# Second attention of a four-layer network: one written order of slots, with score, maximum and exponential as separate steps

## The reference, cut to what matters

```
xn = layernorm(x)                                  # 2 x 1024 x 256
q = rope(xn @ Wq.T)                                # 16 heads of 128
k = rope(xn @ Wk.T); v = xn @ Wv.T                 # 4 heads of 128, each for 4 query heads
g = sigmoid(xn @ Wgslc.T) + sigmoid(xn @ Wgswa.T)  # one number per token and head
p = softmax(q @ k.T / sqrt(128) + causal mask)
x = x + (g * (p @ v)) @ Wo.T
```

## Time and profile before

| | |
|---|---|
| median of three runs | 3405.4 us |
| the profiled execution, its own time | 3405.0 us |
| its span, first to last instruction | 3403.2 us |
| second attention, first score to the next stage's first product | 735.89 to 1728.80 us |
| mean granted clock of TensorE, all stages | 0.913 |
| busy: TensorE, VectorE, ScalarE, GpSimd | 2888.8, 1793.9, 912.8, 732.8 us |

### The profile page before, as it was taken

The page is one execution under the profiler, slowest core; times in us unless marked ns, Lnnn a source line. Parts: engine busy times, 40 slices in busy tenths (PEclk is TensorE's granted clock), DMA queues, the critical chain, the costliest instruction groups (busy, mean ns, idle before and its releaser), DMA issues. The chain is left out here.

```text
span 3403.2 us, 34916 instructions
## 1 busy us (share of the span) xinstructions
PE 2888.8 (85%) x13440; PEld 1767.6 (52%) x13440; DVE 1793.9 (53%) x3555; ACT 912.8 (27%) x1644; POOL 732.8 (22%) x796
## 2 busy tenths in 40 slices
PE   5889889989999999999999548899788886759975
PEld 3556545655555455555455425555455555636653
DVE  5565641156665756665711357777577763322223
ACT  2434441023233323332311022222222223212211
POOL 3221210012222312322200102333123334230020
PEclk8999989979999999999999668999799997759987
DMA  4112201030000000000000200000000000411220
GB/s 127 29 30 47 45 19 50 0 122 0 1 1 1 0 1 0 1 1 13 0 0 0 85 6 13 13 10 10 10 13 10 13 24 10 190 63 49 66 71 36
DMA packets 52932, 100.62 MB, mean 30 GB/s; under 512 B 10080, under 2 KB 34784, under 8 KB 51488
## 3 DMA queue, kind: packets, MB, share of 16 engines
q1 hardware_dynamic: 49176, 88.94, 9.2%
q0 software_dynamic: 3072, 8.39, 0.8%
q10 hardware_dynamic: 520, 1.07, 0.2%
HBM read 54.32 MB, written 18.61 MB: 21 GB/s over the span
## 5 line engine op out<-in xcount | busy, mean ns | idle before, releaser
L1133 ACT ACTIVATE back<-ps,front 128x128 f32<-128x128 f32 (+7 forms) x256 | 189.7, 741 | 617.7 <-DVE front L1175 617.6
L1098 PE MATMUL ps<-back 128*128 128x512 f32 x576 | 296.1, 610 | 67.6 <-DVE back L1194 34.2
L778 DVE TENSOR_REDUCE front<-ps 128x1 f32<-128x512 f32 (+3 forms) x384 | 197.5, 553 | 116.4 <-PE ps L634 88.9
L1744 DVE TENSOR_TENSOR_SCAN back<-ps,back 128x512 f32<-128x512 f32 x128 | 155.6, 1217 | 127.8 <-PE ps L1595 127.8
L1222 POOL TENSOR_SCALAR back<-back,front 128x128 f32<-128x128 f32 (+5 forms) x192 | 143.6, 749 | 324.9 <-DVE front L1184 322.4
L1175 DVE TENSOR_REDUCE front<-ps 128x1 f32<-128x128 f32 (+7 forms) x256 | 194.1, 758 | 8.8
L739 ACT ACTIVATE back<-ps 128x1024 f32<-128x1024 f32 (+1 forms) x192 | 150.0, 809 | 139.1 <-PE ps L656 138.3
L1583 PE MATMUL ps<-front 128*128 128x512 f32 x320 | 160.8, 643 | 29.1 <-ACT back L1686 12.9
L1089 PEld LDWEIGHTS ps<-front,back 128*128 128x128 f32 x1152 | 136.5, 141 | 83.7 <-issue 61.7
L1089 PE MATMUL ps<-front,back 128*128 128x128 f32 x1152 | 163.5, 274 | 4.6 <-DVE back L1166 4.6
L1098 PEld LDWEIGHTS ps<-back 128*128 128x128 f32 x576 | 93.6, 190 | 137.5 <-ACT back L1139 55.9
(11 more groups left out here) (304 smaller groups left out, 5547.2 us busy)
## 6 DMA issues: line engine op xcount, KB each, us to landing
whole<-l_w SPq DMA_DIRECT2D x32, 512.0 KB, 12.9
front<-back SPq DMA_DIRECT2D x128, 64.0 KB, 2.0
rounded<-rounded SPq DMA_DIRECT2D x120, 64.0 KB
rounded<-front SPq DMA_DIRECT2D x120, 64.0 KB
xg<-front SPq DMA_DIRECT2D x1, 6016.0 KB, 31.9
front<-xg SPq DMA_DIRECT2D x47, 128.0 KB, 2.1
yg<-front SPq DMA_DIRECT2D x47, 128.0 KB, 1.7
front<-l_win SPq DMA_DIRECT2D x1, 4640.0 KB, 14.0
```

Source lines behind the costliest of these rows:

```text
L778: e.tensor_reduce(self.nm[u % 2][:, r, t, h:h + 1], self.bank(step)[:, 0:n], AX.X, ALU.max, negate=True).then_inc(D.sem, 1)
L1098: e.matmul(PS[:, 7, :], self.V[:, j, G % 4 * 128:G % 4 * 128 + 128], self.turned(("turn", n, j)), start=(j == 0), stop=(j == qt)).then_inc ...
L1133: e.activation(self.P[n % 2][:, h, :nk], s[:, :nk], ACT.Exp, bias=st[:, 0, h:h + 1], scale=1.0, accum_out=st[:, 1, h:h + 1]).then_inc(A.se ...
L1744: e.tensor_tensor_scan(m.LT[:, h, four, :].rearrange("p a b -> p (a b)"), self.bank(step, self.B), m.ident4, 0.0, ALU.mult, ALU.add).then_ ...
```

## The change

The order is written anew. Every head of every unit has two **slots**, 8 per unit. Block j of unit n is turned at slot 8n + 10 + 8j // (qt + 1) and multiplied two slots later, so that the last blocks of a unit are turned and multiplied beside the unit after the next. The copy of a block turned at an odd slot is ScalarE's, at an even slot VectorE's (`by_act`).

Score, maximum and exponential are steps of their own, *score*, *max* and *exp*. In a head's even slot stand in order: score, the projection or output product that belongs here, a turn, a mul, the *end* of the previous head, and this head's *max*. In its odd slot: a turn, a mul, and *exp*. Behind both stand the steps *rope* (the rotation) and *sum* (the addition to x) of a projection or output product. The step *o* is a step too, and for a group's first unit it is held until the last output product of the group before. The projections and output products are spread one to a head, where before they stood together behind a unit's first score. Two waits are new in form: `wait_banks` has other distances, and the maximum no longer waits for the transposes of the unit before the last, but the gate for GpSimd's scaling there.

```diff
-            if qt == 1:
-                out = [("out", G - 1, i) for i in (0, 2, 4, 6) if G > 0]
-                return out + [("v", 1, i) for i in range(8) if G == 4] + make(G, 1, (-1,))
-            if qt in (2, 3):
-                return make(G, 1, (2 * qt - 4, 2 * qt - 3))
-            return make(G + 1, 0, {5: (-1, 0), 6: (1, 2), 7: (3,)}.get(qt, ()))
...
-        for n, (G, qt) in enumerate(units):
-            for h in range(4):
-                order.add("score", n, h)
-                if end:
-                    order.add(*end)
-                end = ("end", n, h)
...
+        turn, mul, beside = {}, {}, {}
+        for n, (G, qt) in enumerate(units):
+            for j in range(qt + 1):
+                slot = 8 * n + 10 + 8 * j // (qt + 1)
+                turn[slot] = ("turn", n, j)
+                mul[slot + 2] = ("mul", n, j)
...
+        for G in range(8):
+            for i in range(4):
+                put(G + 1, *((1, 2), (1, 3), (2, 0), (2, 1))[i], ("out", G, 2 * i))
+            for h, (qt, at) in zip(range(-1, 4), ((1, 0), (2, 0), (2, 1), (3, 0), (3, 1))):
+                put(G, qt, at, ("proj", G, 1, h))
+            for h, (qt, at) in zip(range(-1, 4), ((5, 0), (5, 2), (6, 0), (6, 2), (7, 0))):
+                if G < 7:
+                    put(G, qt, at, ("proj", G + 1, 0, h))
+        put(4, 1, 2, *[("v", 1, i) for i in range(8)])
...
+        for n in range(67):
+            for h in range(4):
+                late = []
+                for half in range(2):
+                    slot = 8 * n + 2 * h + half
+                    if half == 0:
+                        if n < 64:
+                            order.add("score", n, h)
+                        for s in beside.get(slot, ()):
+                            order.add(*s)
+                            if s[0] == "proj":
+                                late.append(("rope",) + s[1:])
+                            if s[0] == "out":
+                                late.append(("sum",) + s[1:])
+                                if s[2] == 6 and held:
+                                    order.add(*held)
+                                    held = None
+                    if slot in turn:
+                        order.add(*turn[slot])
+                    if slot in mul:
+                        order.add(*mul[slot])
+                        _, m, j = mul[slot]
+                        if (m % 8, m // 8 > 0) == (0, True):
+                            held = ("o", m)
+                        elif j == units[m][1]:
+                            order.add("o", m)
+                    if half == 0:
+                        m, k = (n, h - 1) if h else (n - 1, 3)
+                        if 0 <= m < 64:
+                            order.add("end", m, k)
+                        if n < 64:
+                            order.add("max", n, h)
+                    elif n < 64:
+                        order.add("exp", n, h)
+                for s in late:
+                    order.add(*s)
+
+        self.by_act = {s: slot % 2 == 1 for slot, s in turn.items()}
...
-        i = 4 * n + h - (4 if q < 16 else 3 if q == 16 else 2)
+        i = 4 * n + h - (2 if q == 0 or q > 16 else 3 if q in (1, 2, 16) else 4)
...
-                self.slot[step] = ring.take("d", step)
+                self.slot[step] = ring.take("d", ("rope",) + step[1:])
...
+                if n > 1 and h < 3:
+                    w.wait_ge(self.pooled, self.gn["end", n - 2, h])
```

More of the change, by code:

```diff
@@ L941, in plan @@
-        order.add(*end)
-        for s in rest + now + [("out", 7, i) for i in (0, 2, 4, 6)]:
-            order.add(*s)
+        for h in range(-1, 4):
+            order.add("proj", 0, 0, h)
+            order.add("rope", 0, 0, h)
+        held = None
+        for n in range(67):
+            for h in range(4):
+                late = []
[12 more added lines that the diff above has]
+                                    order.add(*held)
+                                    held = None
+                    if slot in turn:
[17 more added lines that the diff above has]
+                    order.add(*s)
@@ L980, in plan @@
             elif kind == "turn":
-                self.slot[step] = ring.take("a" if order.no[step] % 2 == 0 else "d", step)
+                self.slot[step] = ring.take("a" if self.by_act[step] else "d", step)
                 p.add(*step)
-                (a if order.no[step] % 2 == 0 else d).add(*step)
+                (a if self.by_act[step] else d).add(*step)
             elif kind == "mul":
                 p.add(*step)
-                if step[2] == units[step[1]][1]:
-                    a.add("o", step[1])
             elif kind == "out":
-                self.slot[step] = ring.take("d", step)
+                self.slot[step] = ring.take("d", ("sum",) + step[1:])
                 p.add(*step)
+            elif kind == "sum":
                 d.add(*step)
@@ L1139, in act @@
                     e.activation(self.turned(step), self.bank(step), ACT.Copy).then_inc(A.sem, 1)
-            elif kind == "mul" and step[1:] == self.last(step[1]):
-                G, qt = self.units[step[1]]
-                w.wait_ge(self.products, self.pn[step])
+            elif kind == "o":
+                n = step[1]
+                G, qt = self.units[n]
+                w.wait_ge(self.products, self.pn["mul", *self.last(n)])
                 if G > 0:
@@ L1190, in dve @@
             elif kind == "turn":
-                if self.order.no[step] % 2 == 1:
+                if not self.by_act[step]:
                     w.wait_ge(self.products, self.pn[step])
@@ L1194, in dve @@
                     e.tensor_copy(self.turned(step), self.bank(step)).then_inc(D.sem, 1)
-            elif kind == "out":
+            elif kind == "sum":
                 _, G, i = step
                 x = X[:, G // 4 * 8 + i:G // 4 * 8 + i + 2, :]
-                w.wait_ge(self.products, self.pn[step])
-                e.tensor_tensor(x, x, self.bank(step).rearrange("p (a b) -> p a b", a=2), ALU.add).then_inc(D.sem, 1)
+                w.wait_ge(self.products, self.pn["out", G, i])
+                e.tensor_tensor(x, x, self.bank(("out", G, i)).rearrange("p (a b) -> p a b", a=2), ALU.add).then_inc(D.sem, 1)
     @property
     def parts(self):
-        return [s for s in self.order.steps if s[0] == "proj"]
+        return [s for s in self.order.steps if s[0] == "rope"]
     def pool(self, e, w):
```

52 lines of the change are left out of this document (18 added, 34 removed).

## The result

The changed kernel takes 3430.0 us in the median of four runs (3425.81 to 3432.86); the kernel before, with a fourth run, 3405.8. The ratio is 1.0069, interval 1.0052 to 1.0087: slower by 0.7%, where 3423 was forecast. The profiled execution took 3427.41 us, and its span of 3425.7 lies 22.5 us above that of before.

What follows compares the result with a forecast made beforehand. TensorE, busy 85%, was taken as the bound. In a 122.3 us group, 12.2 us of waits would give way to 15.0, making 125.1; over all groups +19, rounded to +18: 3423 us, range 3372 to 3442.

Steps and rivals of the forecast that it cites:

- the removed ones: TensorE's waits in a group, mostly products waiting for copies, that the change takes away: 12.2 us with hidden parts.
- the walk: Following one head group instruction by instruction in the new order: new waits of 15.0 us, a group of 125.1.
- block 7's first transpose: In the stretch of qt = 7, this transpose waits 0.5 us for the fourth head's end.
- blocks 2 and 3: Stretches of qt = 2 and 3: VectorE needs 22.4 us against TensorE's 16.3, so TensorE loses 6.1.
- waits for a rotation: Banks held until VectorE rotates a projection, blocks 1, 5, 6, 7: 6.0 us a group; idle expected at about 8.
- the sum: Second attention stage: group increases of 2.7 us, 2.5 in group 0 and 0.7 in the last, together +19 us.
- The last step of the sum: Whole kernel: the stage's +19 us rounded to +18, giving 3423.
- Blocks 3 and 4: Stretches of qt = 3 and 4 in a group: about 15.5 and 10.7 us forecast.
- The rule on bubbles: Repeated TensorE gaps can mean too little SBUF or PSUM; with three banks bubbles only move, a group staying at 122 us.
- B: Rival: two slots of slack let VectorE's queue hide the rotations; a group 115 us, kernel 3350, or 3378 at half; chance 0.26.
- C: Rival: the chain's waits and the removed ones cancel within 7 us, a group staying at 121.5 to 123.2; chance 0.16.
- D: Rival: the chain of maximum, exponential and end costs in every block; a group adds 8 us, kernel 3480; chance 0.03.

Runs made afterwards that it cites:

- e4: Changed kernel with the rotation's exchange of halves left out, two VectorE instructions instead of three; ratio to the kernel before 0.9903.
- e3: Changed kernel with the projection behind the turn and the mul on TensorE within an even slot; ratio to the kernel before 0.9892.
- e10: Changed kernel with GpSimd's addition that completes a rotation replaced by a scaling by one; ratio to the kernel before 1.0001.
- e9: Changed kernel with the edits of e3 and e8, copies left by slot; 3338.0 us, ratio to the kernel before 0.9795.
- e6: Changed kernel with the edits of e3, e5 and e8 together; median 3323.9 us, ratio to the kernel before 0.9757.
- e7: Changed kernel with a block multiplied one slot behind its turn instead of two, except each group's first unit; ratio to the kernel before 1.0291.
- e1: Changed kernel with each head's maximum ahead of the previous head's end, in all heads; ratio to the kernel before 0.9979.
- e8: Changed kernel with the maximum ahead of the previous head's end in heads 1 to 3 only; ratio to the kernel before 0.9978.
- e5: Changed kernel with e3's edit, and all copies of turned blocks of units qt = 1 to 3 on ScalarE; ratio to the kernel before 0.9910.

## Why the prediction was right, point by point

**The sign and the mechanism held.** Waits of a length the removed ones had came back on VectorE's queue. In group 6 they are, in the order of the walk, with the 0.17 us that each hides: 0.44 at block 7's first transpose (0.5 predicted), 1.62 in block 1 (1.8), 0.43 at the output product (0.4), 1.56 in block 5 (1.7), 1.55 in block 6 (1.7), 0.68 in block 7 (0.8). In blocks 2 and 3 the product waits 2.33 + 0.17 for a copy behind a rotation (2.3). All waits for a rotation come to 6.0 us idle a group, where about 8 were forecast. If 2.0 us are small gaps as before, waits cost a group 14.2; 15.0 were predicted: 124.3 against 125.1. e4 shows that the bank waits are caused as the prediction said: a rotation 0.7 us shorter takes 0.8 from each, with the takings unchanged. e3 agrees, but moved the takings too.

**The stage was over-counted by 3 us, the kernel under-counted by 7.** The stage grew by 15.7 us, where the sum had 19. The last group gained nearly all back (142.5 against 142.2; +0.7 was predicted), group 0 lost 4.2 rather than 2.5, groups 1, 2, 5 and 6 lost 2.0 each and group 4 2.9, and group 3 0.3, since a stretch at half speed had lengthened it before (124.0). The other 6.8 us in the profiled executions are in stages that the change doesn't touch; no term of the prediction covered them. So 3423 lies 7 us under 3430 through what no term covered, while its own mechanism was over-counted; the two partly cancel, which is luck. The last step of the sum, from +19 to +18, has no reason given.

**Blocks 3 and 4, forecast too short.** For block 3, 15.5 us was forecast and for block 4, 10.7: 26.2. They take 27.4. The idle time forecast around them held better in sum: 6.1 for blocks 2 and 3 and 1.6 for block 4 are 5.1 and 2.4 in group 6, hidden parts included. How 15.5 and 10.7 follow from it the prediction does not show. What it left out is that VectorE's gate stands still while GpSimd's addition runs. Timeline of group 5, block 3, GpSimd's addition and VectorE's reciprocal and gate:

```profile
1397.64 1.27 POOL L1244 TENSOR_TENSOR back<-back 128x512 f32<-128x512 f32 x1 [2.80 <-DVE back L1196]
...
1397.79 1.14 DVE L1214 TENSOR_TENSOR front<-back,front 128x1 f32<-128x1 f32 x1
...
1406.20 1.27 POOL L1244 TENSOR_TENSOR back<-back 128x512 f32<-128x512 f32 x1 [4.69 <-DVE back L1196]
1406.75 0.15 DVE L1209 RECIPROCAL front<-front 128x1 f32<-128x1 f32 x1
1406.94 0.54 DVE L1214 TENSOR_TENSOR front<-back,front 128x1 f32<-128x1 f32 x1
```

The gate, 0.16 us elsewhere, ends at 1398.93 and 1407.48, the additions at 1398.91 and 1407.47. A rotation now stands right ahead of a copy and a gate, so that its addition falls on the gate more often: the gate's mean is 269 ns against 188 before, 21 us of VectorE in the stage, where its busy time grew by 18 beyond the copies. Of the 256 gates 61 are drawn longer than 0.25 us (24 before), and each of these ends within 0.02 us of the end of a GpSimd instruction; the reciprocal, with one input, keeps its 0.15 to 0.16 us even inside an addition. In block 3 the gates are lengthened by 1.7 us, 0.5 before: about the 1.2 by which the forecast is short. e10 takes the addition away and gets 1.4 us a group back. The Trainium skill (SBUF — State Buffer, SBUF: two separate sides) states this: a VectorE operation with two SBUF inputs and a GpSimd operation that reads SBUF take the shared port pair in turn, each for its whole length. The trace agrees.

**The rule on bubbles.** The Trainium skill's rule on repeated gaps (Perfetto Trace Analysis, Optimization Strategy), weighed in the prediction, was read there as keeping a group at 122 us with three banks, the bubbles moved. e3, e9 and e6 keep the three banks and have 117.0, 113.4 and 111.5, so the waits could be taken away without another bank, by when one was given back and asked for. Whether a fourth bank would have done it too, no run here shows. The Trainium skill (Perfetto Trace Analysis, Matmuls) counsels rotating groups over banks so that the evacuation of one overlaps the next; the changed kernel did so and still waited 6.0 us a group, where VectorE's queue evacuated a bank late.

**The rivals.** B, faster by two slots of slack, failed on the point named for it: the product of block 3 still waits 2.33 us for a copy. Its ground was not empty, since e7 loses 9.5 us a group with one slot. C fell by 1 us a group. D, the chain costing in every block, is excluded: block 7, which has the longest chain, loses 0.7 us in one wait, for a rotation.

## What to carry to other kernels

Where an engine's queue is written by hand, ask of each instruction at its head what its producer still has to do first: a copy that waits for transposes behind a projection held up a ready maximum and a rotation, and with it the bank that TensorE wanted. Putting work whose result is needed late behind the work whose result is needed soon, on the producer, was worth 7 us of 124 without touching the work of the engine that looked overloaded; it also put off the next use of the bank, and the two were not tried apart. Try such edits together too: copies given to an idle engine were worth 0.7 us in the stage while what ran ahead of them was late, and 16.2 once it was not.

## What the runs showed of the hardware that was not expected

**A stretch of slower TensorE clock that cost a group nothing.** In group 5 block 3 had a granted clock of 0.92 and took 17.80 us; in group 6 it had 1.00 and 16.47:

```profile
1520.43:1536.90 16.47, 12.02 (x36) 5.03 (x35) 15.04 (x33) 3.39 (x9) 6.35 (x7) 1.00 0.00 0
1536.90:1547.80 10.90, 9.03 (x36) 4.68 (x35) 7.78 (x22) 5.18 (x12) 2.29 (x3) 1.00 0.01 2
```

Blocks 3 and 4 together take 27.36 and 27.37 us, both groups 124.32. The half speed (1.2 of 2.4 GHz) fell on the end of block 3, behind the late copy: two products took 2.07 us there and 1.12 in group 6. Block 4 got it back, since its scores came later and TensorE waited there 0.9 us for an exponential and not 1.9 for exponentials and a copy. Before, a stretch of half speed in block 3 cost 1.7 us: group 3's length was 124.04 us where its neighbours' were 122.3.

**Untouched stages change in length.** The second feed-forward part, the third and the fourth layer, before and after:

```profile
1728.80:1926.18 197.38, 172.97 (x545) 103.54 (x545) 40.05 (x93) 26.66 (x42) 11.92 (x20) 0.92 0.09 37
1926.18:2975.16 1048.98, 846.11 (x5450) 542.62 (x5450) 668.23 (x1002) 247.51 (x348) 292.53 (x240) 0.87 0.08 25
2975.16:3403.20 428.04, 325.32 (x1206) 208.88 (x1206) 118.24 (x283) 77.42 (x182) 61.89 (x64) 0.81 0.18 59
```

```profile
1743.49:1940.83 197.34, 172.69 (x544) 103.42 (x544) 40.07 (x93) 26.66 (x42) 11.92 (x20) 0.94 0.09 37
1940.83:2993.93 1053.10, 849.52 (x5450) 543.96 (x5450) 667.98 (x1002) 247.43 (x348) 292.05 (x240) 0.87 0.08 25
2993.93:3425.69 431.76, 330.70 (x1206) 211.61 (x1206) 118.09 (x283) 77.40 (x182) 61.75 (x64) 0.80 0.18 58
```

The same instructions took 1674.4 and 1682.2 us. Over the profiles of e1 to e9, which share this code, they took from 1673.7 (e8) to 1688.3 us (e5). These layers run at a mean granted clock of 0.80 to 0.94, so what part of them falls into the half-speed stretches can differ. That this makes the difference is argued from the clock alone; no run here held it fixed. A change of 0.2% in such a kernel is read from the length of the changed stage, and not from the total.
